# An eight-stage graph network and expert kernel: how edges are marked and in what order stages hand over

## The chip, the cores and the metric

The kernel runs on one core of one Trainium2 chip. The metric is device time in microseconds (us). Each number under "time" is one whole execution of the kernel; the median of three is given. One further execution was recorded by the profiler, and all rows come from it.

## What is computed

A residual network of four blocks over 1250 nodes with 1024 features each. The 21250 edges are sorted by destination. `LN` is a layer norm without scale and offset.

```python
# block 1: 4 hops of attention over the edges (row = source, col = destination)
x1  = LN(x) @ W1 + b1                                  # 1250 x 512
dis = clip(number of edges into a node, 1) ** -0.5
gnn = x1
for k in range(4):
    alpha = tanh(gnn[col] @ Wi[k] + gnn[row] @ Wj[k] + bg[k])       # one number an edge
    msg   = (dis[row] * dis[col])[:, None] * alpha[:, None] * gnn[row]
    gnn   = gnn + segment_sum(msg, col)
x = x + concat([x1, gnn], 1)
# block 2: dense layer, and for each node the best of 4 low-rank experts
x = x + LN(x) @ W.T + gate * (LN(x) @ Wd[top1].T @ Wu[top1].T)
# block 3: two layers of  h @ W_self + mean over incoming edges(h) @ W_neigh + b, relu between
x = x + sage(relu(sage(LN(x))))
# block 4: 8 experts; each takes its 313 best nodes by a router's softmax
for e in range(8):
    x[sel[e]] += gate[e] * (gelu(LN(x)[sel[e]] @ w1[e] + b1[e]) @ w2[e] + b2[e])
```

## The kernel before, in words

**Tiles.** Nodes stand in 10 tiles of 128 rows (padded to 1280). Weights and activations that are multiplied are split into two f16 parts, a high and a low one; a product of such pairs is three matmuls (high x high, low x high, high x low). Five instruction streams run beside one another and wait by semaphores: TensorE (`pe`), VectorE (`v`), ScalarE (`s`), GpSimd (`g`) and SyncE, whose stream issues most transfers.

**First stage (A).** For each node tile: layer norm (`ln` on ScalarE, coefficients on VectorE, low part `ln_low_a` on GpSimd), 16 transposes, 24 matmuls of 512 columns with W1 and 16 small ones with the attention vectors (`v1s`). Between the tiles' products stand the windows, from which the adjacency matrix is counted. A window is 50 destination nodes; 25 windows cover 1250. Edges lie in 170 chunks of 125. For each chunk a marking matrix is made twice: `oh_d` (125 edges x 500, one column for each pair of source tile and destination in the window) on VectorE by comparing a row of numbers (`iotaw`) with a code for each edge, and `oh_s` (125 x 128, the place of the source in its tile). A matmul of the two adds the chunk's edges into a bank of 500 columns. The code of an edge depends on the window: GpSimd works out 170 of them for each window (L672 to L674, three instructions). `oh_s` is made on ScalarE for three chunks of four (distance L1399, then L1408 or L1419) and on VectorE for the fourth (L1732). A window takes 4 chunks at first and 4 more in each further visit of a loop whose count is read from a table (L571 to L575): 27 visits in all. A last product with zeros (L1034) closes the bank, and ScalarE copies it into `adj` (L1425).

**Hops.** The adjacency matrix is dense: 10 source tiles x 1280 destinations. A hop is done in two halves of five destination tiles. For each source tile ScalarE makes tanh of the attention sum over 640 destinations (`th`, L1450), VectorE multiplies by the counts (`hm`, L1790), ScalarE copies to the high part (`hop`, L1455) and VectorE subtracts to the low part (L1795). TensorE does 150 products a half (L1075 to L1077) and, ahead of them, `chain` (L1097), 80 small products that bring the new attention sums; their row is copied by VectorE (`prow`, L1832), spread by TensorE (L1124). After each half the new features are formed on VectorE and ScalarE (L1804, L1462, L1808). `dinv_row` (1280 columns) is a reciprocal that the sums by destination are scaled with (L1827). Ahead of the first hop stand the degrees: a square root (L1472), the scaling of the first features (L1479) and the row of attention sums (L1439). From the first hop on GpSimd also loads and converts the weights of block 2 (`whole(a["ffnW"] ...)`, L645 to L647).

**Later stages.** Block 2 (B) and block 3 (C) follow with the same two-part products (L1159 to L1198) and statistics (L512); the order of steps at their borders is written out by hand in `staged_late` and `flow_late`. At the border of B and C the gates `zT` (L1959) come from VectorE, and tile 0 of C is loaded as `cx` by SyncE's queue (L856), behind the loads and stores of B (L808, L852). The router of block 4 has a chain of its own a tile: statistics, coefficients (L521 to L532), ScalarE `cy` (L544) and its f16 copy `dyh` (L547), GpSimd's low part (L536), transposes (L556).

## Time and profile before

| what | value |
|---|---|
| median of three runs | 1720.75 us (1716.56 to 1721.64) |
| the profiled execution | 1721.65 us, span 1720.0 us, mean granted TensorE clock 0.94 |
| TensorE matmul busy (PE) | 1515.6 us, 88% of the span |
| weight load (PEld, beside PE) | 813.7 us |
| VectorE (DVE) | 918.1 us, 53% |
| ScalarE (ACT) | 632.5 us, 37% |
| GpSimd (POOL) | 386.2 us, 22% |
| transfers | 158.16 MB, mean 92 GB/s |

The span is what the profiler's records cover; 1.65 us of the execution lie outside. A busy share is an average over the stages. The first 230 us hold the first stage and the way to the hops, about 229 to 580 the four hops, then B, from 730 C, from about 1390 the experts. In each row a name stands as out<-in by the program's names, xN is a count of instructions, and what stands behind `<-` in brackets is what released an engine that had been idle.

### The profile page before, as it was taken

Reading aid. Unit: us, or ns where it says so; the run is one execution under the profiler, and the core shown is the slowest. Engines: PE = TensorE matmul, PEld = TensorE weight load, DVE = VectorE, ACT = ScalarE, POOL = GpSimd, SP = SyncE. Lnnn points to the kernel's source line nnn. Section 1 sums busy time; section 2 is a strip of 40 time slices with the busy share of each in tenths; the row PEclk is TensorE's granted clock in tenths of the full one; section 3 lists DMA queues with packets and bytes.
Section 4 is the critical chain, followed back from the end, with each engine's and each line's share of the span. In section 5 each row is a group of like instructions: output and inputs, shape, how many; then the busy total and the mean of one; then the engine's idle time right before and its main releaser. Section 6 shows DMA issues by size and latency. Waiting matters only on the chain.

```text
span 1720.0 us, 30722 instructions
## 1 busy us (share of the span) xinstructions
PE 1515.6 (88%) x9054; PEld 813.7 (47%) x9054; DVE 918.1 (53%) x2102; ACT 632.5 (37%) x858; POOL 386.2 (22%) x355
## 2 busy tenths in 40 slices
PE   5788767799999998789999998999988925999996
PEld 4344334344445454344445444444544524766764
...
DMA packets 55685, 158.16 MB, mean 92 GB/s; under 512 B 6980, under 2 KB 8467, under 8 KB 55608
## 3 DMA queue, kind: packets, MB, share of 16 engines
...
q14 instruction: 36, 0.29, 0.1%
...
## 4 chain that ended last, share of the span: by engine, by line
PE 47%; issue 26%; DVE 13%; ACT 6%; POOL 3%; DMA 2%; ACTq 1%; DVEq 1%; SPq 0%; POOLq 0%
PE ps L1159 12%; PE ps L1346 7%; PE ps L1330 6%; PE ps L1230 5%; PE ps L1075 2%; PE ps L1076 2%; PE ps L1077 2%; PE ps L996 2%; PE ps L556 2%; DVE hm L1790 2%; ACT th L1450 2%; DVE gn L1804 1%; PE ps L1318 1%; DVE bstat L512 1%; POOL wa L647 1%
## 5 line engine op out<-in xcount | busy, mean ns | idle before, releaser
L1159 PE MATMUL ps<-wa,tb 128*128 128x512 f16 x960 | 214.3, 384 | 6.9 <-DVEq L2083 5.2
L1230 PE MATMUL ps<-adj,nm 128*128 128x512 f16 (+1 forms) x960 | 178.5, 345 | 2.9 <-DVEq L2042 1.6
L1075 PE MATMUL ps<-gp,hop 128*128 (+1 forms) x400 | 154.4, 386 | 29.7 <-DVE hop L1795 18.6
L1076 PE MATMUL ps<-gp,hop 128*128 (+1 forms) x400 | 154.0, 385 | 0.0
L1077 PE MATMUL ps<-gp,hop 128*128 (+1 forms) x400 | 153.9, 385 | 0.0
L1159 PEld LDWEIGHTS ps<-wa,tb 128*128 (+1 forms) x960 | 93.8, 99 | 119.6 <-issue 10.9
L1230 PEld LDWEIGHTS ps<-adj,nm 128*128 x960 | 93.4, 97 | 88.4 <-issue 4.4
L1547 ACT ACTIVATE tb<-cx 128x512 f32 (+1 forms) x48 | 26.8, 559 | 282.5 <-DVE cx L2032 282.5
L1346 PE MATMUL ps<-wa,hT 128*105 128x512 f16 x576 | 126.8, 379 | 1.7 <-issue 1.7
L1159 PE MATMUL ps<-wb,hop 128*128 128x512 f16 x480 | 109.2, 389 | 0.0
L1159 PE MATMUL ps<-wa,hop 128*128 128x512 f16 x480 | 106.6, 383 | 2.9 <-DVEq L1969 2.9
L1330 PE MATMUL ps<-tkT,wb 128*128 128x315 f16 x768 | 106.6, 300 | 1.1 <-ACT tkT L1593 1.1
L1159 PE MATMUL ps<-wb,tb 128*128 128x512 f16 x480 | 106.1, 385 | 1.4 <-ACT tb L1500 1.4
L1731 DVE TENSOR_SCALAR oh_d<-iotaw,code 125x500 f16 (+1 forms) x208 | 75.0, 422 | 43.1 <-POOL code L674 37.3
L1346 PEld LDWEIGHTS ps<-wa,hT 128*105 128x105 f16 x576 | 72.6, 128 | 50.2 <-issue 2.0
L1330 PEld LDWEIGHTS ps<-tkT,wb 128*128 128x128 f16 x768 | 75.2, 98 | 32.1 <-issue 1.3
L1790 DVE SCALAR_TENSOR_TENSOR hm<-adj,th 128x640 f32<-128x640 f32 x80 | 68.9, 903 | 37.0 <-ACT th L1450 35.6
L2032 DVE TENSOR_TENSOR cx<-ps,dinv_row 128x512 f32<-128x512 f32 (+1 forms) x48 | 29.0, 603 | 110.7 <-PE ps L1230 110.7
L536 POOL TENSOR_TENSOR dyh<-cy,dyh 128x1024 f16<-128x1024 f32 x10 | 21.2, 2124 | 271.5 <-ACT dyh L547 271.5
L1075 PEld LDWEIGHTS ps<-gp,hop 128*128 (+1 forms) x400 | 40.0, 100 | 78.6 <-issue 34.1
L1795 DVE TENSOR_TENSOR hop<-hm,hop 128x640 f32 x80 | 69.3, 908 | 13.7 <-ACT hop L1455 13.7
L1159 PEld LDWEIGHTS ps<-wb,tb 128*128 x480 | 47.5, 99 | 59.8 <-issue 4.7
...
## 6 DMA issues: line engine op xcount, KB each, us to landing
w_st<-in_ew SPq DMA_DIRECT2D x16, 2048.0 KB, 11.1
...
```

The costliest lines, as they stand in the source:

```text
L556: ins = pe.transpose(bank16(bank + part)[:, k * P:k * P + TP], y_[:, k * P:(k + 1) * P], ident16[0:TP, 0:TP])
L996: pe.matmul(ps[:, 2 + j, :], lhs, w1[:, w, k, :], start=(n == 0), stop=(n == 3 * KT - 1))
L1075: pe.matmul(acc, wh, gh, start=(s_ == 0), stop=False, skip_group_check=True)
L1076: pe.matmul(acc, wh, gl, start=False, stop=False, skip_group_check=True)
L1077: ins = pe.matmul(acc, wl, gh, start=False, stop=(s_ == NT - 1), skip_group_check=True)
L1159: ins = pe.matmul(ps[:, b + c, :], lhs(part, k), w[:, w_, k, c * 512:(c + 1) * 512], start=(k == 0 and part == 0 and w_ == 0), stop=(last ...
L1230: ins = pe.matmul(ps[:, 6 + j, 0:w_], nm[:, part, s_, bass.ds(f * P, P)], adj[:, s_, CC * c:CC * c + w_], start=(s_ == 0 and part == 0), s ...
L1330: ins = pe.matmul(ps[:, 2 + h, 0:3 * SLOT], w1b[:, j, w_, k * H + h * P:k * H + (h + 1) * P], tkT[:, j, part, k, :], start=(k == 0 and w_ ...
L1346: ins = pe.matmul(ps[0:SLOT, 6 + o, :], hT[:, part, h, c * SLOT:(c + 1) * SLOT], w2b[:, j, w_, h * D + o * 512:h * D + (o + 1) * 512], sta ...
L1731: v.tensor_scalar(dst[:, c], iotaw[:], at[:, c:c + 1], None, ALU.is_equal)
L1790: v.scalar_tensor_tensor(hm[:, j, :], tile_of(adj[:, :, h * HALF:(h + 1) * HALF], 2 * r + j), 2.0, th[:, j, :], ALU.mult, ALU.mult).then_i ...
L1795: v.tensor_tensor(tile_of(hop[:, h, 1], 2 * r + j).rearrange("p (d n) -> p d n", n=P)[:, :, 0:TP], hm[:, j, :].rearrange("p (d n) -> p d n ...
```

## The change

**Marks.** GpSimd's codes are gone. VectorE works out once, at the start, one number an edge (`key`, which holds window, source tile and place in the window); one number a window (`winbase`) comes from the index row. An edge is marked by one instruction with two per-partition numbers: `(iotaw + winbase[w]) is_equal key`. A window takes 6 chunks at first and 2 more in each visit (again 27 visits); ScalarE makes `oh_s` for 4 of the 6, VectorE for 2 of the 6 and for both of a visit. The last product of a window closes its bank, without the product with zeros.

**The first stage's order.** Windows are 2 a tile for the first five tiles and 3 a tile for the last five (`WINDOWS`). ScalarE writes the high part of the normed tile straight from `xt`; GpSimd makes the full one and the low one. The loads of W1 come in another order, the statistics of the tiles are spread over the stage, the small products with `v1s` stand between groups of others, degrees are counted in three parts.

**Seam to the hops.** The square root of the source scale is made on VectorE, five tiles first; GpSimd scales the first features (high part); the first half hop's tanh and products are written out right behind the last window, and ahead of the table loads and clamps. The reciprocal of `dinv_row` is done on 128 columns, and on 384 more in each of three hops. New features go copy by copy, with the low part one step behind. The weight conversion of GpSimd waits for its turn: a pair of slices each hop (`hop_turn`).

**Borders of B and C, router.** `staged_late` and `flow_late` have their steps in another order, and the router's chain takes `dyh` from ScalarE's first pass, while GpSimd makes `cy` and the low part. Its coefficients take three linked instructions fewer.

The order of instructions on VectorE in one window of the first stage, before: four marks `oh_d` and one `oh_s`, then the loop of visits with four marks and one `oh_s` each.

```order
L1731 TENSOR_SCALAR oh_d<-iotaw,code 125x500
L1732 REGISTER_ALU
L1732 TENSOR_SCALAR oh_s<-iota,slo 125x128
...
L1731 TENSOR_SCALAR oh_d<-iotaw,code 125x500
L1731 ISA
L1731 TENSOR_SCALAR oh_d<-iotaw,code 125x500
L1731 ISA
L1731 TENSOR_SCALAR oh_d<-iotaw,code 125x500
L1731 ISA
L1731 TENSOR_SCALAR oh_d<-iotaw,code 125x500
L1732 ISA
L1732 TENSOR_SCALAR oh_s<-iota,slo 125x128
```

The same place now. The marking matrix is printed as `wa`, since it lies in that tile's storage.

```order
L1778 TENSOR_SCALAR wa<-iotaw,winbase,key 125x500
L1780 REGISTER_ALU
L1780 TENSOR_SCALAR oh_s<-iota,slo 125x128
L1780 REGISTER_ALU
L1780 TENSOR_SCALAR oh_s<-iota,slo 125x128
...
L1778 TENSOR_SCALAR wa<-iotaw,winbase,key 125x500
L1778 ISA
L1778 TENSOR_SCALAR wa<-iotaw,winbase,key 125x500
L1780 ISA
L1780 TENSOR_SCALAR ohv_s<-iota,slo 125x128
L1780 ISA
L1780 TENSOR_SCALAR ohv_s<-iota,slo 125x128
```

Of the marks ahead of the loop only the last is shown. Four marks and one `oh_s` by VectorE became six and two, and a visit's four and one became two and two.

ScalarE from the last window to the hops, before: the eviction `adj`, a table load, the root `dis`, the scaling of five tiles of features `gp`, then the loop with its clamps, and the tanh `th` behind another table load.

```order
L1425 ACTIVATE adj<-ps 128x10x50 x2
L1472 ACT_TABLE_LOAD
L1472 ACTIVATE dis<-dcol 128x10
L1479 ACTIVATE gp<-gn,dis 128x512 x5
L1446 UNCONDITIONAL_BRANCH
L1446 ISA
L1450 ISA
L1450 ACT_TABLE_LOAD
L1450 ACTIVATE th<-arow,bcur 128x640
L1449 REGISTER_ALU
L1450 ISA
L1450 ACTIVATE th<-arow,bcur 128x640
```

The same place now:

```order
L1460 ACTIVATE adj<-ps 128x10x50
L1467 ACTIVATE arow<-ps 128x512 x2
L1467 ACTIVATE arow<-ps 128x256
L1460 ACTIVATE adj<-ps 128x10x50
L1473 ACTIVATE th<-arow,bcur 128x640 x2
L1478 ACTIVATE hop<-hm 128x640 x2
L1473 ACTIVATE th<-arow,bcur 128x640 x2
L1478 ACTIVATE hop<-hm 128x640 x2
L1473 ACTIVATE th<-arow,bcur 128x640 x2
L1478 ACTIVATE hop<-hm 128x640 x2
```

Root and features left ScalarE, the copies of the row of attention sums (`arow`) stand between the last two evictions, and the pairs of tanh and high part follow at once.

TensorE at the border of B and C, before. L1159 are the dense products, L1198 the low-rank experts (`zT` is the gate times the down product), L1191 the transposes of that, L556 the transposes of the next stage's input.

```order
L1191 MATMUL ps<-ident,zcat 48x128
L1159 MATMUL ps<-wa,hop 128x512 x48
L1198 MATMUL ps<-wus,zT 128x512 x2
L556 MATMUL ps<-ident,nm 128x128 x16
L1191 MATMUL ps<-ident,zcat 48x128
L1198 MATMUL ps<-wus,zT 128x512 x2
L1159 MATMUL ps<-wb,hop 128x512 x48
L556 MATMUL ps<-ident,nm 128x128 x16
L1159 MATMUL ps<-wb,hop 128x512 x48
```

The same place now (L1217 were L1159, L1256 L1198, L1249 L1191, L585 L556):

```order
L1249 MATMUL ps<-ident,zcat 48x128
L1217 MATMUL ps<-wa,hop 128x512 x48
L1256 MATMUL ps<-wus,zT 128x512 x2
L1249 MATMUL ps<-ident,zcat 48x128
L585 MATMUL ps<-ident,nm 128x128 x16
L1256 MATMUL ps<-wus,zT 128x512 x2
L1217 MATMUL ps<-wb,hop 128x512 x48
L585 MATMUL ps<-ident,nm 128x128 x16
L1217 MATMUL ps<-wb,hop 128x512 x48
```

The last transposed gate moved ahead of the transposes of C's first tile, so that these stand between it and the product that reads `zT`.

SyncE's queue there, before: stores of a tile (L852) and loads of the next (L808) in turn, then the first tile of C, `cx`.

```order
L852 DMA x_d<-cr 128x1024
L808 DMA cr<-x_d 128x512
L808 DMA cr<-xg_d 128x512
L852 DMA x_d<-cr 128x1024
L808 DMA cr<-x_d 128x512
L808 DMA cr<-xg_d 128x512
L860 DMA bias<-in_bs 128x1024
L856 DMA cx<-x_d 128x1024 x2
L852 DMA x_d<-cr 128x1024
```

The same place now (L901 was L852, L857 L808, L909 L860, L905 L856):

```order
L901 DMA x_d<-cr 128x1024
L857 DMA cr<-x_d 128x512
L857 DMA cr<-xg_d 128x512
L909 DMA bias<-in_bs 128x1024
L905 DMA cx<-x_d 128x1024 x2
L901 DMA x_d<-cr 128x1024
```

The loads of `cx` stand one store earlier than before.

The diff, cut to the parts that are spoken of:

```diff
-GC = 4
+GC, GV = 6, 2
+GA = 4
 PAIRS = NCH // 2
 assert PAIRS * 2 == NCH
-BATCHES = ((0, 2), (2, 6), (6, 10))
+BATCHES = ((0, 2), (2, 4), (4, 7), (7, 10))
+LOADS = ((0, 2), (2, 4), (4, 10))
 HALF = 5 * TP
 PROJ = 256
...
+WINDOWS = tuple(range(2 * t, 2 * t + 2) if t < 5 else range(3 * t - 5, 3 * t - 2) for t in range(NT))
...
-    tr_n(0, 0), ln_n(0, 1), work(last, 1)
-    stats_n(1), tr_n(0, 1), ln_n(1, 0), done_n()
-    for step, lag in steps:
-        if lag == 1:
-            step(last, 1)
+    tr_n(0, 0), ln_n(0, 1), work(last, 1), done_n()
+    ends = [step for step, lag in steps if lag == 1]
+    for step in ends[:-1]:
+        step(last, 1)
+    tr_n(0, 1)
+    for step in ends[-1:]:
+        step(last, 1)
+    stats_n(1), ln_n(1, 0)
...
-    store(2, 1), again(3, 0), store(3, 0), again(3, 1), ahead(0), store(3, 1), again(4, 0), ahead(1)
+    store(2, 1), again(3, 0), ahead(0), store(3, 0), again(3, 1), store(3, 1), again(4, 0), ahead(1)
...
-                step.link(v.tensor_tensor(z2, z, z, ALU.mult))
-                step.link(v.tensor_tensor(z2, z2, ve, ALU.mult))
+                if single:
+                    step.link(v.scalar_tensor_tensor(z2, z, ve, z, ALU.mult, ALU.mult))
+                else:
+                    step.link(v.tensor_tensor(z2, z, z, ALU.mult))
+                    step.link(v.tensor_tensor(z2, z2, ve, ALU.mult))
...
             def ln_low_a(t):
-                ln_low(g, A, 0, t, y, yh[:, t % 2, :], yl[:, t % 2, :])
+                j = t % 2
+                g.wait_ge(A.aff, 1 + sum(t >= t1 for _, t1 in BATCHES))
+                g.tensor_scalar(y[:, j, :], xt[:, t, :], lnv_a[:, 1, t:t + 1], lnv_a[:, 2, t:t + 1],
+                                ALU.mult, ALU.add).then_inc(A.y, 1)
+                g.wait_ge(A.y, t + 1)
...
-            def codes(w):
-
-                j = w % 2
-                if w >= 2:
-                    g.wait_ge(s_win, w - 1)
-                link(g.tensor_scalar(ctmp[:, j, :], dst_f[:], winneg[0:EP, w:w + 1], -1.0, ALU.add, ALU.max))
-                link(g.tensor_scalar(ctmp[:, j, :], ctmp[:, j, :], float(WIN), None, ALU.min))
-                g.tensor_tensor(code[:, j, 0:NCH], ctmp[:, j, :], shw[:], ALU.add).then_inc(s_code, 1)
-
...
+            def hop_turn(r):
+                if isinstance(r, int):
+                    g.wait_ge(s_hlo, NT * (2 * HOPS - 1) + 2)
+                else:
+                    g.wait_ge(s_abc, r + 2)
+                    g.sem_inc(s_tick, 1)
 
             g.wait_ge(s_hlo, 2 * NT + 2)
-            whole(a["ffnW"], wa, s_wf)
+            whole(a["ffnW"], wa, s_wf, turn=hop_turn)
...
+                    g.wait_ge(D_.aff, D_.r + 2 * r + j + 1)
+                    g.sem_inc(s_tick, 1)
+                    g.wait_ge(D_.lo, D_.m + 2 * r + j)
+                    g.sem_inc(s_tick, 1)
+                    g.tensor_scalar(cy[:, 0, :], cr[:, j, :], lnv[:, 1, j:j + 1], lnv[:, 2, j:j + 1],
+                                    ALU.mult, ALU.add).then_inc(D_.y, 1)
+                    g.wait_ge(D_.y, D_.n + 2 * r + j + 1)
+                    g.sem_inc(s_tick, 1)
...
-                pe.matmul(acc, zero16[:, 0:P], zero16[:], start=False, stop=True, skip_group_check=True).then_inc(s_win, 1)
-
-            turn_a(0)
...
+            turn_a(0)
+            for t in range(NT):
+                products(t)
+                if t == 7:
+                    degrees(0, 5, ps[:, 4, 200:210])
+                for w in WINDOWS[t]:
+                    if w == NWIN - 1:
+                        pe.wait_ge(s_abc, 1)
+                        broadcast_a((0, 1, 3))
+                        degrees(5, 8, ps[:, 2, :])
+                    window(w)
+                    if w == WINDOWS[t][0] and t + 1 < NT:
+                        turn_a(t + 1)
+            degrees(8, NT, ps[:, 2, :]), row_degrees()
...
             def ln(t):
-                j = t % 2
                 s.wait_ge(A.aff, 1 + sum(t >= t1 for _, t1 in BATCHES))
-                s.activation(y[:, j, :], xt[:, t, :], ACT.Identity, scale=lnv_a[:, 1, t:t + 1],
-                             bias=lnv_a[:, 2, t:t + 1]).then_inc(A.y, 1)
-                s.wait_ge(A.y, t + 1)
-                s.activation(yh[:, j, :], y[:, j, :], ACT.Copy).then_inc(A.hi, 1)
+                s.activation(yh[:, t % 2, :], xt[:, t, :], ACT.Identity, scale=lnv_a[:, 1, t:t + 1],
+                             bias=lnv_a[:, 2, t:t + 1]).then_inc(A.hi, 1)
 
...
+                for c in range(GA):
+                    ins = s.activation(dist[:, j, c, :], iota128[:], ACT.Abs, scale=-1.0, bias=at[:, c:c + 1])
+                ins.then_inc(s_dist, 1)
+                if w >= 2:
+                    s.wait_ge(s_win, w - 1)
                 s.wait_ge(s_dist, w + 1)
-                s.activation(oh_s[:, j, 0:GC - 1], dist[:, 0], ACT.Relu, scale=-1.0, bias=1.0).then_inc(s_ohs, 1)
...
+            s.wait_ge(s_A_st[0], 16 * 6)
+            for s_ in range(0, NT, 2):
+                tanh_of(s_, s_ % 2, 0, s_), tanh_of(s_ + 1, 1, 0, s_ + 1)
...
-                v.tensor_scalar(shw[:], shi[:], float(CW), 1.0, ALU.mult, ALU.add).then_inc(s_shw, 1)
...
+                link(v.scalar_tensor_tensor(key[:, 0:NCH], shi[:], float(CW), rest[:], ALU.mult, ALU.add))
+                link(v.scalar_tensor_tensor(key[:, 0:NCH], q_f[:], float(NT * CW), key[:, 0:NCH], ALU.mult, ALU.add))
...
-                def visit(chunk, dst, src):
-                    at, lo = code[:, j, bass.ds(chunk, GC)], slo[:, bass.ds(chunk, GC)]
-                    for c in range(GC):
-                        v.tensor_scalar(dst[:, c], iotaw[:], at[:, c:c + 1], None, ALU.is_equal)
-                    return v.tensor_scalar(src[:, GC - 1], iota128[:], lo[:, GC - 1:GC], None, ALU.is_equal)
-
-                v.wait_ge(s_code, w + 1)
+                def marks(chunk, n, n_s, dst, src):
+                    at, lo = key[:, bass.ds(chunk, n)], slo[:, bass.ds(chunk, n)]
+                    for c in range(n):
+                        v.tensor_scalar(dst[:, c], iotaw[:], winbase[0:EP, w:w + 1], at[:, c:c + 1], ALU.add, ALU.is_equal)
+                    for c in range(n_s, n):
+                        ins = v.tensor_scalar(src[:, c], iota128[:], lo[:, c:c + 1], None, ALU.is_equal)
...
-                visit(first, oh_d[:, j], oh_s[:, j]).then_inc(s_ohd, 1)
+                    v.wait_ge(s_win, w - 1)
...
+            edges(), stats(0, 2), coefficients(0), ranges()
             for c in range(4):
                 w1_low(c)
-            split_v1(), ranges()
...
+                for w in WINDOWS[t]:
+                    if w + 2 < NWIN:
+                        one_hots(w + 2)
+                if t == 0:
+                    stats(4, 7), coefficients(2)
+                if t in (1, 2, 3):
+                    stats(6 + t, 7 + t)
+                if t == 3:
+                    coefficients(3)
+                if t == 8:
+                    first_features(0, 5)
...
+            for s_ in range(0, NT, 2):
+                product_of(s_, 0, 0, s_), product_of(s_ + 1, 1, 0, s_ + 1)
+                low_of(s_, 0, 0, s_), low_of(s_ + 1, 1, 0, s_ + 1)
+                if s_ == 2:
+                    take_degrees(3, 5, NT, ps[0:TP, 2, :])
+                if s_ == 4:
+                    source_scale(5, NT)
+            first_features(5, NT)
...
+                evict(0)
+                for d in range(1, 5):
+                    evict(d)
                     if split:
-                        v.wait_ge(s_ghi, 10 * (k + 1) + t + 1)
-                        ins = v.scalar_tensor_tensor(tile_of(gp2[:, 1], ring * NT + t), gn[:, t, :], dis16[:, t:t + 1],
-                                                     tile_of(gp2[:, 0], ring * NT + t), ALU.mult, ALU.subtract)
+                        low(d - 1)
                 if split:
-                    ins.then_inc(s_gp, 1)
-
-            v.sem_inc(s_gev, 5)
-            v.sem_inc(s_hm, 2)
...
-            link(v.reciprocal(dinv_row[:], dinv_row[:]))
-            with step.loop(0, HOPS - 1, 5) as k:
+            v.wait_ge(s_rest, 1)
+            link(v.reciprocal(dinv_row[:, 0:P], dinv_row[:, 0:P]))
...
+                part = dinv_row[:, bass.ds(k * (3 * P) + P, 3 * P)]
+                link(v.reciprocal(part, part))
...
-                ln_coefficients(v, step, D_, mv[:, j:j + 1, :], lnv[:, :, j:j + 1])
+                ln_coefficients(v, step, D_, mv[:, j:j + 1, :], lnv[:, :, j:j + 1], True)
```

## Rows read from the trace of the kernel before

**Rows 1.** Busy time by stretches; columns: stretch, length, PE, PEld, DVE, ACT, POOL, PEclk, DMA, GB/s

```profile
41.00:181.00 140.00, 113.54 (x722) 55.10 (x720) 101.25 (x291) 100.80 (x220) 71.32 (x78) 0.93 0.06 20
...
229.00:362.50 133.50, 113.41 (x560) 52.36 (x563) 97.60 (x113) 64.27 (x90) 43.46 (x32) 0.90 0.10 32
362.45:434.99 72.54, 71.31 (x407) 34.29 (x407) 46.81 (x72) 37.86 (x53) 0.00 (x0) 1.00 0.00 0
```

**Rows 2.** VectorE's waits, 40 to 206; columns: us in total, times, longest.

```profile
DVE oh_d L1731 <- POOL code L674: 37.3, 11, 5.9
```

**Rows 3.** ScalarE's groups, 40 to 206; columns: busy us, mean ns, idle before.

```profile
L1399 ACT ACTIVATE dist<-iota,slo 125x128 f16 x81 | 26.7, 391 | 1.8 <-issue 0.4
L1425 ACT ACTIVATE adj<-ps 128x500 f16<-128x500 f32 x25 | 14.4, 577 | 21.3 <-PE ps L1034 21.2
L1376 ACT ACTIVATE y<-xt,lnv_a 128x1024 f32<-128x1024 f32 x8 | 9.8, 1231 | 2.2 <-DVE lnv_a L532 2.2
```

**Rows 4.** VectorE's timeline, marks; columns: start, duration.

```profile
124.69 1.11 DVE L1731 TENSOR_SCALAR oh_d<-iotaw,code 125x500 f16<-125x500 f16 x4
...
131.70 2.21 DVE L1731 TENSOR_SCALAR oh_d<-iotaw,code 125x500 f16<-125x500 f16 x4 [3.33 <-POOL code L674]
```

**Rows 5.** VectorE's timeline, two pointers and two tensors.

```profile
384.76 1.56 DVE L1795 TENSOR_TENSOR hop<-hm,hop 128x640 f32 x2 [0.32 <-ACT hop L1455]
...
1395.81 0.23 DVE L2100 TENSOR_SCALAR sc<-rtmp 128x8 f32<-128x8 f32 x1
1396.08 0.29 DVE L2126 TENSOR_SCALAR sc<-sc,live 128x8 f32<-128x8 f32 x1
```

**Rows 6.** TensorE's groups, 40 to 206, products with W1.

```profile
L996 PE MATMUL ps<-wa,yT 128*128 128x512 f16 x240 | 60.1, 390 | 0.0
```

**Rows 7.** Timeline of all engines, last window to first hop.

```profile
203.85 0.59 ACT L1425 ACTIVATE adj<-ps 128x500 f16<-128x500 f32 x1 [1.83 <-PE ps L1034]
...
218.31 1.28 ACT L1450 ACT_TABLE_LOAD   x1
...
223.03 1.28 ACT L1450 ACT_TABLE_LOAD   x1
...
228.88 0.60 PE L1075 MATMUL ps<-gp,hop 128*128 x1 [18.55 <-DVE hop L1795]
...
242.20 8.15 DVE L1827 RECIPROCAL dinv_row<-dinv_row 128x1280 f32<-128x1280 f32 x1
```

**Rows 8.** Timeline of TensorE and VectorE in the hops.

```profile
268.57 6.08 PE L1097 MATMUL ps<-hop,pp 128*32 128x384 f16 x80 [5.11 <-DVE hop L1795]
...
305.52 2.98 DVE L1795 TENSOR_TENSOR hop<-hm,hop 128x640 f32 x2 [0.31 <-ACT hop L1455]
...
362.45 3.43 PE L1097 MATMUL ps<-hop,pp 128*32 128x384 f16 x80
...
370.46 0.86 PE L1124 MATMUL ps<-sel,prow 128*128 128x32 f32 x6 [1.23 <-DVE prow L1832]
```

**Rows 9.** TensorE's waits, 206 to 362.

```profile
PE ps L1075 <- DVE gn L1804: 11.1, 1, 11.1
```

**Rows 10.** TensorE's waits, 670 to 729.

```profile
PE ps L1198 <- DVE zT L1959: 15.5, 2, 8.7
```

**Rows 11.** Timeline at the border of B and C.

```profile
678.34 2.49 DVE L512 BATCH_NORM_STATS2 bstat<-cx 128x6 f32<-128x512 f32 x4 [9.74 <-DMA cx<-x_d]
...
716.45 12.84 PE L1159 MATMUL ps<-wb,hop 128*128 128x512 f16 x48
```

**Rows 12.** TensorE's waits, 1276 to 1392.

```profile
PE ps L556 <- POOL dyh L536: 13.6, 2, 9.2
```

**Rows 13.** ScalarE's timeline in the router.

```profile
1384.84 1.24 ACT L544 ACTIVATE cy<-cr,lnv 128x1024 f32<-128x1024 f32 x1 [8.04 <-DVE lnv L532]
1386.11 1.06 ACT L547 ACTIVATE dyh<-cy 128x1024 f16<-128x1024 f32 x1
```

**Rows 14.** GpSimd's groups, whole span.

```profile
L645 POOL TENSOR_SCALAR stage<-stage 128x1024 f32<-128x1024 f32 x32 | 37.6, 1175 | 16.2 <-DMA stage<-in_wn 6.5 <-DMA stage<-in_ws 3.6 <-DMA stage<-in_ffnW 3.0
```

505 lines of the change are left out of this document (268 added, 237 removed).

## The prediction, made before the change was run

> **What bounds the kernel now.** I read the busy shares by stage first. Up to 204 us (the first stage: layer norm, first product, adjacency matrix) TensorE is busy for 114 of 140 us, VectorE and ScalarE for 101 each [rows 1]: nobody is full, all wait for one another in turn. In the first hop it is 113 in 133.5 [rows 1]; between the two lies a seam in which it stands nearly still. Then the waits, and the timeline where a wait is long. In the first stage VectorE waits 37.3 us for the codes of GpSimd [rows 2], and a window costs ScalarE six absolute distances of 0.39 us, two roundings and an eviction of 0.58 [rows 3]. So the stage ends by ScalarE and by VectorE waiting for codes, the hops by TensorE, once they run: from one chain product to the next 72.54 us, of which TensorE is busy 71.31 [rows 1]. Everything after 716 us is left as it was but for the router list.
>
> The profiled execution took 1721.65 us (span 1720.0, so 1.65 around it); the median of the three runs is 1720.75. I sum against 1721.65.
>
> **First stage.** What goes: 25 code triples of GpSimd; two of six distances a window and one rounding pass on ScalarE; the closing product with zeros (one of nine 500-column products); the `y` pass of ScalarE, 1.23 us a tile [rows 3], which GpSimd now makes beside it. What comes: VectorE makes four 128-wide one-hots a window instead of two, so 8 marks and 4 one-hots instead of 8 and 2 (the tables give 27 visits in either kernel: 208 marks before, 204 now).
>
> A mark is 0.28 us undisturbed (four in 1.11) and 0.55 beside GpSimd (four in 2.21) [rows 4]. The new mark reads two per-partition numbers. No row has it at this size. Bounds: nothing more than now, or what a second pointer adds on 8 columns, 0.29 against 0.23 [rows 5]; I take 0.03 for back-to-back issue, half of that, since the difference is partly latency. The far end is the loss of the fast mode: 640 float columns of two tensors took 1.56 for two, 0.78 each [rows 5], so some 0.65 for 500. The Trainium skill, "VectorE: DVE Perf Modes", section "Mode 4×_2P — both tricks at once", lets a second operation sit in slices of its own, so that it costs nothing; no run here shows it for two pointers. By that page the first stage would be 3 us shorter than I sum.
>
> Per tile then. TensorE: the 240 products took 60.1 us with slow stretches in it [rows 6]; 24 of them, by my estimate, 5.4, the small ones, now in a block, 0.4, transposes 1.2 and 1.7 a window: 10.4 with two windows, 12.1 with three. ScalarE: 3.2 a window (4 × 0.39, 0.58 and two roundings of about half a us), 1.0 + 1.23 for the tile [rows 3]: 8.7 or 11.9. VectorE: 2.9 a window, 0.7 + 0.7 + about 1.2 of statistics, some 2 for GpSimd's 4.7 us of work: 10.4 or 12.1. All three are level, and a third window must wait for its marks, which VectorE starts only after the transposed tile: 14 a tile. Start: the products began at 41 us, where the first stretch of [rows 1] does; VectorE must now work through keys, statistics, ranges, four weight parts of 1.23 and the first transposes: 38. First tile 6, then two of 15 (11, and 4 for the filling of the pipeline and the statistics of four tiles), to 74; three tiles of 11 to 107; four of 14, and 3 for degrees and features, to 166; the last windows with the broadcast 9; eviction and second pointers 3: last window evicted at 178. It was at 203.85 + 0.59 = 204.4 [rows 7]. **−26.4.** If the engines never waited for one another it would be 165; if the interleaving gains nothing over today's average of 14 a tile, 195.
>
> **Seam to the hops.** From that eviction to the first hop product, 228.88, it was 24.4 us [rows 7]: square root with its table load, feature scaling, row clamp, then three pairs of tanh and product. The root goes to VectorE beside it, the features to GpSimd, the first half hop is written out ahead of the clamps. A pair took 223.03 − 218.31 = 4.72, 1.28 of it a table load [rows 7], which the order has no more: 3.44. Three pairs, the first filling, 12.9. **−11.5.** Who comes late next: the second five sources need their features, at some 26 us after the eviction; TensorE is then on the first five until 31 (12.9, 16.2 for 75 products, 2 slow). Covered by 5.
>
> **Hops.** From the first product at 228.88 to the chain of the next hop at 362.45 it was 133.6 [rows 7, 8]. An undisturbed hop is 72.54 [rows 1], half a hop's 150 products (72.54 less the chain's 3.43 [rows 8] and some 4.5 of small ones, halved) 32.3: 104.8. The excess, 28.8, is the waits of 11.1 [rows 9] and 5.1 [rows 8], a shorter one, and slow clock after each: the same chain took 6.08 there and 3.43 here [rows 8]. The 5.1 comes from the reciprocal of 8.15 [rows 7] ahead of the second half; now 128 of 1280 columns stand there and 384 after each hop's columns (2.5). The 11.1 comes from GpSimd's weight conversion beside the next half: two subtractions took 2.98 [rows 8] instead of 1.56 [rows 5]. The conversion is spread: a pair of slices (12 us) after each hop's columns. SBUF — State Buffer in the Trainium skill, section "Who interferes with whom", has a VectorE operation with two SBUF inputs and a GpSimd one exclude each other for whole instructions; the trace agrees, by that doubling. So each pair still lies some 6.5 us on the next half: 3.4 later, but VectorE has 8 in hand there, since the features now go evict, evict, low without waiting for ScalarE (7 us for five, was 12.6). I leave 3 for the cold start: −25.8, and the row-copy wait of 1.23 [rows 8] in two later hops, which now has two products' blocks before it: −2.5. **−28.3.**
>
> **Seam from B to C.** TensorE waits twice for `zT`, 15.5 together [rows 10]. First 8.7: VectorE stood 9.74 for the load of `cx` [rows 11], which SP issued behind a store; that load moves ahead of the store of tile 7, ready 12 us earlier, so nothing waits, and the slow instructions behind it (1.6) go. Then 6.8: statistics were in front of the `zT` copy; they now follow it, and 48 products that took 12.84 after the idling [rows 11] take 10.5, by 0.215 each as in a hop. Together 19.8; the low part of the next tile is then just in time, for which I leave 0.8. **−19.**
>
> **Router.** TensorE waits for `dyh` twice, 13.6 [rows 12]; elsewhere the list is covered by 10.5 us of products. The chain loses the second pass (1.06 [rows 13]) and three linked operations of 0.2 on eight columns or fewer, as the 0.23 [rows 5]; GpSimd's multiply-add beside ScalarE's own 1.24 [rows 13] can at best be as fast as that and at worst 0.5 later (mean of the like in GpSimd 1.18 [rows 14]). 1.65 twice: **−3.3.** Each of the two could be up to 0.5 worse.
>
> Sum −26.4 − 11.5 − 28.3 − 19.0 − 3.3 = −88.5: **1633 us**.
>
> **Rivals.** (1) The first stage stays coupled: windows wait for marks in every tile, last window at 195 instead of 178. For it: three engines within 10% of each other, and 4.7 us of GpSimd a tile. Against: the long waits for codes are gone. 1650. (2) The conversions cost more than the slack: each of three hops 3.4 to 6 on the path, and the last pair lies on the last half hop, another 3. For it: TensorE is 98% busy in a hop, so all that is late shows. Against: VectorE is busy only 46.8 of 72.5 us there. 1648. (3) Marks at one column a cycle, 0.65: 204 × 0.37 = 75, less 15 for the slack that VectorE has in ScalarE's and TensorE's shadow: 1693. For it: a form that no row shows; against: the page above. (4) Slower: the same place, priced higher. VectorE starts each mark only when both pointers are read and the last mark has drained, 0.29 [rows 5] and an estimated 0.52 for 500 columns (the 0.65 above less latency), 0.81. From 0.80 a mark the sum is not negative: (88.5 + 15)/204 = 0.51 over 0.28. At 0.85 it is 1733. (5) The seams move on: the wait at `zT` is found again at the next tile's low part, and only half of the 19 comes: 1643.
>
> **Chances.** Forecast 0.58, (1) 0.14, (2) 0.10, (3) 0.06, (4) 0.03, (5) 0.09. The likeliest one's own range is 1615 to 1648 (stage end 168 to 188, seams and hops 5 either way). All unknown ends together, without (3) and (4) and the thin tails: 1608 to 1672. A measurement tells 0.3% (5 us): faster 0.95, same 0.02, slower 0.03; only (4) and something unseen of like size lie beyond.
>
> **What would show it.** First stage: no codes, VectorE's marks at 0.26 to 0.32 undisturbed, last adjacency eviction at 168 to 188. Seam: tanh right behind it, no table load in the first half hop, first hop product 13 later. Hops: no TensorE wait over 2 us between first hop product and last, and about 284 us of them in all. Seam B to C: no idle on VectorE for `cx` and both `zT` waits under 1 us. Router: last `dyh` wait near 7.5 instead of 9.2. I am wrong if marks take 0.4 or more alone, if TensorE waits for a half hop's low parts while GpSimd converts, or if the last eviction is later than 195.

## The result and the profile after

The changed kernel took 1677.3 us (median of four, 1671.2 to 1677.9), the kernel before 1719.8 in runs beside it: a ratio of 0.9747, with a 95% interval of 0.972 to 0.9774. It is 42 us faster where the forecast's sum was 88.5, and the time lies outside the range given, 1608 to 1672. The profiled execution has a span of 1675.9 us.

To see where the 44 us of the two spans come from I cut both at the same six instructions. Times are starts in the traces, in us (the products of C are taken to their end); the forecast's figure stands in the last column. An eviction is the copy of a finished bank of TensorE's results; the last one into `adj` ends the first stage.

| from ... to | before | after | change | forecast |
|---|---|---|---|---|
| start, last eviction into `adj` | 203.9 | 211.8 | +7.9 | −26.4 |
| that, first hop product | 25.0 | 11.3 | −13.7 | −11.5 |
| that, first dense product of B | 315.6 | 287.7 | −27.9 | −28.3 |
| that, end of C's products with its first `W_self` | 296.9 | 291.0 | −5.9 | −19.0 |
| that, last small product of the router | 551.6 | 546.8 | −4.8 | −3.3 |
| that, end | 327.0 | 327.3 | +0.3 | 0 |

Four rows came within 2.5 us of the forecast. Two did not, and they are the whole miss: the first stage by 34 us, the border of B and C by 13 (the others together gave 3 us more than forecast).

**The first stage.** Stretches of the profile after: start and end, length, then busy time and instructions of PE, PEld, DVE, ACT and POOL, the granted TensorE clock, DMA share, GB/s.

```profile
41.00:181.00 140.00, 101.76 (x644) 47.05 (x642) 120.17 (x321) 61.07 (x129) 45.98 (x28) 0.83 0.04 16
122.40:142.40 20.00, 15.80 (x82) 6.81 (x80) 14.88 (x38) 9.29 (x21) 5.10 (x3) 0.74 0.04 15
223.10:508.00 284.90, 281.87 (x1550) 134.87 (x1551) 224.35 (x335) 144.06 (x197) 51.78 (x37) 0.99 0.14 44
```

In the same 140 us VectorE is busy for 120 us instead of 101 [rows 1], ScalarE for 61 instead of 101, and TensorE for less, 102 instead of 114: the work that left ScalarE was not what held the stage. The second line is one tile with three windows: 20 us, where I had summed 14, at a granted clock of 0.74 of full speed. The third holds the four hops. The waits of TensorE up to 520 us (total, times, longest) name what it stood for:

```profile
PE ps L1051 <- DVE yT L592: 19.9, 4, 7.9
PE ps L1081 <- DVE oh_s L1780: 16.6, 6, 8.8
...
PE ps L1087 <- DVE ohv_s L1780: 6.1, 5, 2.4
```

All three are for VectorE: copies of the transposed tile (`yT`) and one-hots, with the marks ahead of them. (The only other one of that size is for a load of W1, ahead of 41 us.) A stretch of the timeline without GpSimd, then that tile, VectorE and GpSimd (start, duration):

```profile
99.98 2.00 DVE L1778 TENSOR_SCALAR wa<-iotaw,winbase,key 125x500 f16<-125x500 f16 x6
...
124.31 0.41 DVE L1780 TENSOR_SCALAR oh_s<-iota,slo 125x128 f16<-125x128 f16 x2
125.20 2.14 POOL L566 TENSOR_TENSOR yl<-y,yh 128x1024 f16<-128x1024 f32 x1 [12.41 <-ACT yh L1434]
125.28 3.34 DVE L1780 TENSOR_SCALAR ohv_s<-iota,slo 125x128 f16 x2
127.31 1.26 POOL L705 TENSOR_TENSOR xt<-xt,gn 128x512 f32<-128x512 f32 x1
128.54 2.86 DVE L1778 TENSOR_SCALAR wa<-iotaw,winbase,key 125x500 f16<-125x500 f16 x6
128.55 1.75 POOL L698 TENSOR_SCALAR y<-xt,lnv_a 128x1024 f32<-128x1024 f32 x1
```

Undisturbed, six marks take 2.00 us and the next instruction starts 1.92 after the first: 0.32 each, against 0.26 to 0.28 [rows 4]. The whole VectorE work of a window is 3.2 us (99.98 to 103.19), where I had 2.9. Two one-hots take 0.41 alone and 3.34 while GpSimd subtracts and adds: the first 2.12 beside the subtraction of 2.14, the second 1.30 beside the addition of 1.26. The next six marks take 2.86 beside its third pass.

The longest wait of the stage stands between the products of the eighth tile and of the ninth, where VectorE also works out the root of the source scale (the first line is its start) and GpSimd scales five tiles of features:

```profile
164.37 0.16 DVE L1828 TENSOR_SCALAR dtmp<-dtmp 128x5 int32<-128x5 int32 x1
...
168.30 5.48 DVE L1778 TENSOR_SCALAR wa<-iotaw,winbase,key 125x500 f16<-125x500 f16 x6 [1.50 <-issue]
...
171.32 8.10 POOL L709 TENSOR_SCALAR gp<-gn,dis 128x512 f16<-128x512 f32 x5
...
174.21 2.24 PE L1081 MATMUL ps<-wa,oh_s 125*128 125x500 f16 x5 [8.80 <-DVE oh_s L1780]
```

The step from tile to tile is 26.9 us there (152.1 to 179.0). The forecast had 3 us for degrees and features in all.

**Seam to the hops.** ScalarE and TensorE after the last window:

```profile
211.81 0.59 ACT L1460 ACTIVATE adj<-ps 128x500 f16<-128x500 f32 x1 [2.01 <-PE ps L1091]
212.30 1.54 ACT L1473 ACTIVATE th<-arow,bcur 128x640 f32<-128x640 f32 x2
215.44 1.53 ACT L1473 ACTIVATE th<-arow,bcur 128x640 f32<-128x640 f32 x2
...
223.14 0.39 PE L1127 MATMUL ps<-gp,hop 128*128 x1 [4.60 <-DVE hop L1809]
```

The tanh follows the eviction at once, a pair of them repeats after 3.14 us without a table load (4.72 with it [rows 7]), and the wait of 18.55 [rows 7] became one of 4.60.

**Hops.** TensorE's waits from the first hop product to B; the first line is the one just shown, ahead of the hops:

```profile
PE ps L1127 <- DVE hop L1809: 4.6, 1, 4.6
PE ps L1127 <- DVE gn L1894: 1.6, 3, 0.6
PE ps L1149 <- DVE hop L1809: 1.4, 1, 1.4
```

The waits of 11.1 [rows 9], 5.11 and 1.23 [rows 8] are gone.

**Border of B and C.** TensorE's waits from 640 to 690, and the timeline behind the last wait for `zT`:

```profile
PE ps L585 <- DVE nm L566: 10.4, 1, 10.4
PE ps L1256 <- DVE zT L2050: 0.8, 1, 0.8
```

```profile
666.02 10.53 PE L1217 MATMUL ps<-wb,hop 128*128 128x512 f16 x48
671.29 1.29 DVE L2057 SCALAR_TENSOR_TENSOR cr<-ps,cr 128x512 f32<-128x512 f32 x2 [5.35 <-DMA cr<-xg_d]
672.80 2.47 DVE L539 BATCH_NORM_STATS2 bstat<-cx 128x6 f32<-128x512 f32 x4 [0.22 <-DVE cr L2057]
681.11 2.12 POOL L678 TENSOR_TENSOR wa<-stage,wa 128x1024 f32 x1 [0.19 <-POOL wa L677]
681.17 2.09 DVE L561 TENSOR_SCALAR lnv<-lnv 128x2 f32<-128x2 f32 x1
687.00 1.89 PE L585 MATMUL ps<-ident,nm 128*128 128x128 f16 x16 [10.44 <-DVE nm L566]
688.68 11.87 PE L1217 MATMUL ps<-wb,hop 128*128 128x512 f16 x48
```

The two waits for `zT`, 15.5 us [rows 10], are 0.8, and a new one of 10.44 stands one tile further. It is followed back in three steps: VectorE's last eviction of B waited 5.35 us for the load of its tile, the statistics of C's next tiles stood behind it, and their small instructions then ran beside GpSimd's weight conversion (2.09 us for two columns). The 48 products behind the wait took 11.87 instead of 10.53.

**Router.**

```profile
PE ps L585 <- POOL dyh L566: 10.1, 2, 8.1
```

It was 13.6 [rows 12]: the two waits are 8.1 and 2.0 where they were 9.2 and 4.4.

### The profile page after: what moved, and what is told of

Same layout as the page of the kernel before. It is cut to its first block, busy times and chain, and to the rows that moved or that the text cites. A ratio compares the mean times of both kernels' runs of the same rounds, so it can differ in the third digit from the quotient of the medians.

```text
span 1675.9 us, 30048 instructions
## 1 busy us (share of the span) xinstructions
PE 1505.0 (90%) x9025; PEld 805.3 (48%) x9025; DVE 958.4 (57%) x2170; ACT 565.2 (34%) x739; POOL 376.2 (22%) x310
## 3 DMA queue, kind: packets, MB, share of 16 engines
q1 hardware_dynamic: 43704, 115.57, 19.4%
## 4 chain that ended last, share of the span: by engine, by line
PE 68%; DVE 16%; issue 8%; ACT 3%; DVEq 2%; DMA 1%; POOL 1%; ACTq 0%; SPq 0%; POOLq 0%
PE ps L1217 24%; PE ps L1288 11%; PE ps L1404 7%; PE ps L1388 6%; PE ps L1127 3%; PE ps L1128 3%; PE ps L1129 3%; PE ps L1051 2%; PE ps L585 2%; DVE hm L1804 1%; DVE wa L1778 1%; PE ps L1376 1%; DVE bstat L539 1%; ACT th L1473 1%; PE ps L1025 1%
## 5 line engine op out<-in xcount | busy, mean ns | idle before, releaser
L1217 PE MATMUL ps<-wa,tb 128*128 128x512 f16 x960 | 214.2, 384 | 6.9 <-DVEq L2174 5.2
L1127 PE MATMUL ps<-gp,hop 128*128 (+1 forms) x400 | 152.6, 381 | 6.2 <-DVE hop L1809 4.6
L1128 PE MATMUL ps<-gp,hop 128*128 (+1 forms) x400 | 152.5, 381 | 0.0
L1129 PE MATMUL ps<-gp,hop 128*128 (+1 forms) x400 | 152.3, 381 | 0.0
L1217 PEld LDWEIGHTS ps<-wa,tb 128*128 (+1 forms) x960 | 93.8, 99 | 119.4 <-issue 10.7
L1288 PEld LDWEIGHTS ps<-adj,nm 128*128 x960 | 93.4, 97 | 88.5 <-issue 4.3
L1217 PE MATMUL ps<-wa,hop 128*128 128x512 f16 x480 | 106.9, 383 | 2.7 <-DVEq L2060 2.7
L1217 PE MATMUL ps<-wb,hop 128*128 128x512 f16 x480 | 107.8, 386 | 0.0
L1217 PE MATMUL ps<-wb,tb 128*128 128x512 f16 x480 | 106.0, 385 | 1.4 <-ACT tb L1531 1.4
L1778 DVE TENSOR_SCALAR wa<-iotaw,winbase,key 125x500 f16<-125x500 f16 (+1 forms) x204 | 85.4, 479 | 8.7 <-issue 8.6
L1051 PE MATMUL ps<-wa,yT 128*128 128x512 f16 x240 | 66.4, 444 | 19.9 <-DVE yT L592 19.9
L2301 DVE SCALAR_TENSOR_TENSOR yb<-ps,adj 105x512 f32<-105x512 f32 x48 | 33.1, 691 | 78.7 <-PE ps L1404 78.7
L1217 PEld LDWEIGHTS ps<-wb,tb 128*128 x480 | 47.4, 99 | 59.7 <-issue 4.6
L1809 DVE TENSOR_TENSOR hop<-hm,hop 128x640 f32 (+1 forms) x80 | 69.0, 902 | 11.8 <-ACT hop L1478 11.5
L1217 PEld LDWEIGHTS ps<-wa,hop 128*128 128x128 f16 x480 | 46.6, 99 | 59.1 <-DVEq L2060 3.2
## 6 DMA issues: line engine op xcount, KB each, us to landing
w_st<-in_ew SPq DMA_DIRECT2D x16, 2048.0 KB, 10.4
```

The lines of the kernel that those rows point to most:

```text
L1051: pe.matmul(ps[:, 2 + j, :], yT[:, j, part, k, :], w1[:, w, k, :], start=(n == 0), stop=(n == 3 * KT - 1))
L1127: pe.matmul(acc, wh, gh, start=(s_ == 0), stop=False, skip_group_check=True)
L1128: pe.matmul(acc, wh, gl, start=False, stop=False, skip_group_check=True)
L1129: ins = pe.matmul(acc, wl, gh, start=False, stop=(s_ == NT - 1), skip_group_check=True)
L1217: ins = pe.matmul(ps[:, b + c, :], lhs(part, k), w[:, w_, k, c * 512:(c + 1) * 512], start=(k == 0 and part == 0 and w_ == 0), stop=(last ...
L1288: ins = pe.matmul(ps[:, 6 + j, 0:w_], nm[:, part, s_, bass.ds(f * P, P)], adj[:, s_, CC * c:CC * c + w_], start=(s_ == 0 and part == 0), s ...
```

## The experiments

All are timed beside the kernel before (1719.4 to 1719.9 us). "Eviction" is the start of the last one into `adj` in the profiled execution. Unless another is named, the edit is made to the changed kernel (1677.3 us, eviction 211.8). Three kernels below are not edited ahead of that eviction and had it at 209.6, 209.9 and 211.4, so a difference of some 2 us in it says nothing.

**The third window's one-hots ahead of the transposed tile.** "One-hots" here are all that VectorE makes for a window, the marks and the 128-wide matrices (function `one_hots`). Theories: O, the order; G, GpSimd stops VectorE; P, the second pointer.

```diff
+                early = t >= 5 and t + 1 < NT
+                if early:
+                    one_hots(WINDOWS[t][0] + 2)
                 if t + 1 < NT:
                     turned(t + 1)
...
-                    if w + 2 < NWIN:
+                    if w + 2 < NWIN and not (early and w == WINDOWS[t][0]):
                         one_hots(w + 2)
```

(and the same on ScalarE, `sources(w + 2)` ahead of `turned(t + 1)`.)

> The changed kernel with one order turned round, in tiles 5 to 8: VectorE and ScalarE make the one-hots of the first of the three next windows before they copy the transposed tile, not behind it. The changed kernel took 1677.3 us; its last adjacency eviction was at 212 us and a tile with three windows took 20 us (122.4 to 142.4). Theory O (order: the marks of the third window stand behind the copy of the transposed tile, so that TensorE, which has only two windows' buffers, waits for them ahead of the products): a tile falls to about 15, the eviction comes at 190 to 195, the kernel takes 1655 to 1660. Theory G (GpSimd's two passes over a tile stop VectorE) and theory P (the second pointer of 204 marks): VectorE's work is the same, so within 5 us of 1677.

Measured 1662.1 us, eviction 198.1: 13.7 of the 34 that were missing, so theory O, if some 3 us less than it said. From one tile's products to the next, from 109.4 on (110.7 in the changed kernel), it took 13.8, 19.4, 16.8 and 20.8 us instead of 19.6, 21.8, 26.9 and 14.8. What is left shows in its timeline: in one tile there is still this.

```profile
135.68 2.18 POOL L566 TENSOR_TENSOR yl<-y,yh 128x1024 f16<-128x1024 f32 x1 [7.50 <-ACT yh L1434]
135.81 3.33 DVE L1783 TENSOR_SCALAR ohv_s<-iota,slo 125x128 f16 x2
...
139.63 0.87 PE L1087 MATMUL ps<-wa,ohv_s 125*128 x2 [3.06 <-DVE ohv_s L1783]
```

**Marks with one pointer.**

```diff
-                        v.tensor_scalar(dst[:, c], iotaw[:], winbase[0:EP, w:w + 1], at[:, c:c + 1], ALU.add, ALU.is_equal)
+                        v.tensor_scalar(dst[:, c], iotaw[:], at[:, c:c + 1], None, ALU.is_equal)
```

> The changed kernel with marks that read one per-partition number instead of two: the window's number is left out, so that only the first window's edges are counted. A mark was 0.32 us undisturbed (six in 2.00 less the overlap) against 0.26 in the kernel before. Theory P: a mark falls back to 0.26, 204 x 0.06 = 12 us, all on the path: 1665. Theory O: VectorE's marks are on the path only where TensorE waits for them, about half: 1671. Theory G: no more than 1671 either, since the stalls stay.

Measured 1672.4, eviction 202.6. The stage gained 9.2 us of P's 12, more than O's half; 4 of them were lost again between B and the end of C's first products (295.1 us instead of 291.0), where nothing was edited. That part lay between 287.1 and 295.1 in all runs of the changed order at that border, and between 277.8 and 278.5 in those where it was turned (below).

**Without GpSimd's two passes over the tile.**

```diff
-                g.tensor_scalar(y[:, j, :], xt[:, t, :], lnv_a[:, 1, t:t + 1], lnv_a[:, 2, t:t + 1],
-                                ALU.mult, ALU.add).then_inc(A.y, 1)
-                g.wait_ge(A.y, t + 1)
-                ln_low(g, A, 0, t, y, yh[:, j, :], yl[:, j, :])
+                g.sem_inc(A.y, 1)
+                g.wait_ge(A.hi, A.m + t + 1)
+                g.sem_inc(A.lo, 1)
```

(and the low part is set to zero once, ahead of the tiles; the addition of 1.26 stays.)

> The changed kernel without GpSimd's full and low part of the normed tile in the first stage (1.75 and 2.14 us a tile): both passes are left out and the low part is zero; semaphores are raised as before. Theory G: VectorE loses its stalls, 3 us twice a tile (two one-hots in 3.34 instead of 0.41): 25 to 35 us earlier, 1645 to 1652. Theory O: the third window still waits behind the copy; what goes is one stall of 3 us on the path in each of five tiles and half of that in the others: 1660 or more. Theory P: no change in marks that are undisturbed.

Measured 1650.6, eviction 189.6: 22.2 us earlier, the kernel 26.7 shorter, as theory G had it. One group of VectorE's from 41 to 213, of this kernel and then of the changed one (count | busy us, mean ns | idle):

```profile
L1780 DVE TENSOR_SCALAR ohv_s<-iota,slo 125x128 f16 x54 | 14.0, 300 | 0.0
```

```profile
L1780 DVE TENSOR_SCALAR ohv_s<-iota,slo 125x128 f16 x54 | 20.5, 421 | 0.0
```

The edit also makes the low part ready sooner, and that could have been the gain. It was not: in the changed kernel the low part was done at least 2.9 us before its transposes began, in every tile (127.3 and 140.4 in the one above). The wait of 8.8 us ahead of the ninth tile's products is still 7.2 here, and GpSimd's scaling of features still runs beside it; no run took that away.

**Two windows a tile, seven at the end.** `WINDOWS` is `2t, 2t+1` for the first nine tiles and all the rest in the last.

> The changed kernel with two windows in each of the first nine tiles and seven behind the last, as the kernel before had it. Theory O: no third window in a tile, tiles of 14 us, the seven last at about 5 us each; last eviction near 202, kernel 1667. Theories G and P: VectorE's work is the same and it is what bounds the stage: last eviction at 212 or later, since the seven last windows have no product beside them; 1677 to 1685.

Measured 1665.7, eviction 199.7. Theory O again: a third window in a tile was worth less than nothing as it was ordered.

**Both edits of the first stage together.** No passes of GpSimd, and the third window's one-hots first.

> The changed kernel with both edits of the first stage: no GpSimd passes over the normed tile (the low part is zero) and the first next window's one-hots ahead of the copy of the transposed tile. Alone they moved the last adjacency eviction from 211.8 to 189.6 and to 198.1. If stalls and order are two causes, the gains add: 176, about where the forecast had put it, and the kernel takes 1677.3 - 26.7 - 15.2 = 1635. If they are one wait seen from two sides, the second adds 5 us or less: eviction at 185 or later, kernel at 1645 or more.

Measured 1638.0, eviction 176.7. The gains add: 22.2 and 13.7 alone, 35.1 together. They are two causes. The marks and one-hots of a window now follow one another without a gap or a stall:

```profile
119.58 2.01 DVE L1781 TENSOR_SCALAR wa<-iotaw,winbase,key 125x500 f16<-125x500 f16 x6 [0.36 <-PE ps L1091]
121.51 0.41 DVE L1783 TENSOR_SCALAR oh_s<-iota,slo 125x128 f16<-125x128 f16 x2
121.83 0.72 DVE L1781 TENSOR_SCALAR wa<-iotaw,winbase,key 125x500 f16 x2
```

**The kernel before with the marks alone.** The diff is the change's own for marks and key; GpSimd's codes are not called, all else is as before.

> The kernel before with one part of the change alone: VectorE marks by one key an edge and the window's number (two pointers), GpSimd makes no codes; visits of four chunks, loads, order, seams and hops are as before. Before: last adjacency eviction at 203.9, kernel 1719.6. Theory F (the 37.3 us that VectorE waited for codes are on the path): it is left with 208 x 0.06 = 12 us more of marks and without the stalls by codes: last eviction near 185, kernel at 1700. Theory C (the stage is coupled; behind the codes the next wait, for TensorE's windows and ScalarE's one-hots, ends 5 us or less earlier): eviction at 197 or later, kernel at 1713 or more.

Measured 1723.2 in ten runs (ratio to before 1.0022, 1.0012 to 1.0031), eviction 205.7: slower, if anything. VectorE's waits from 40 to 206:

```profile
DVE oh_d L1740 <- PE ps L1029: 9.8, 2, 6.2
DVE gn L1714 <- PE ps L998: 8.4, 5, 3.7
DVE oh_d L1740 <- issue: 6.6, 8, 1.4
DVE oh_d L1740 <- PE ps L1020: 6.0, 7, 1.8
```

The wait of 37.3 us for codes [rows 2] is gone, and 24 us of waits for TensorE stand there, where the kernel before had 4.7 (and 3.5 for the degrees at the end of the stage); marks and one-hots are busy for 104 us instead of 90. Theory C held: codes exchanged for marks with two numbers give the stage nothing. What the end of the wait is worth without the dearer marks was not run. One number less a mark gave 9.2 us in the changed kernel, so it may be about that, and not 37.

**The border of B and C: statistics ahead of the last eviction.**

```diff
     tr_n(0, 1)
+    stats_n(1)
     for step in ends[-1:]:
         step(last, 1)
-    stats_n(1), ln_n(1, 0)
+    ln_n(1, 0)
```

> The changed kernel with one step moved at the border of B and C: the statistics of C's tiles 2 and 3 (four of 0.62 us, then the linked coefficients) stand ahead of B's last eviction on VectorE, not behind it. In the changed kernel that eviction waited 5.35 us for a load, the statistics came after it, and TensorE then waited 10.4 us for the low part of C's third tile. From B's first dense product to the end of those of C's first layer it took 291 us. Theory S (order): the wait of 10.4 goes and the slow clock behind it: 279 us, kernel at 1665. Theory W (GpSimd's weight conversion for C, which starts at the same time and stops VectorE's small instructions, is what makes them late): the conversion still meets them, so 4 us at most: 1673.

Measured 1662.9, and 277.8 us for the part that took 291.0: −13.2, theory S, and the part that the forecast had for this border and that was missing. Its timeline:

```profile
663.89 2.45 DVE L540 BATCH_NORM_STATS2 bstat<-cx 128x6 f32<-128x512 f32 x4
...
669.33 1.28 DVE L2058 SCALAR_TENSOR_TENSOR cr<-ps,cr 128x512 f32<-128x512 f32 x2
...
674.41 1.06 PE L586 MATMUL ps<-ident,nm 128*128 128x128 f16 x16
```

The statistics start as the tile's products do (664.04), not 6.8 us behind them, the coefficients are done before GpSimd's conversion begins at 670.58, the eviction finds its load there, and TensorE's transposes stand without a wait. The linked coefficients take 2.9 us there (666.49 to 669.41), 7.9 in the changed kernel beside the conversion (675.43 to 683.32): of the wait of 10.4, 5 us were GpSimd's stalls, met only because the statistics were late.

**The hops: conversion at one stretch.** `whole(a["ffnW"], wa, s_wf)` without `turn=hop_turn`.

> The changed kernel with GpSimd converting the weights of B at one stretch from the first hop on, as the kernel before did, instead of a pair of slices each hop. From the first hop product to B's first dense product it took 287.7 us, before 315.6. Theory H (the conversion stops VectorE, and in the kernel before that was the wait of 11.1 us for new features and the slow clock behind it): the hops take 300 or more, kernel at 1690. Theory E (new features, copied one by one, now come early enough to hide it): 288 to 291, kernel at 1678 to 1681.

Measured 1691.1, hops 302.6 instead of 287.7. TensorE's longest wait from 205 to 560:

```profile
PE ps L1127 <- DVE gn L1894: 15.2, 1, 15.2
```

**The hops: the whole reciprocal first.** `v.reciprocal(dinv_row[:], dinv_row[:])`, and none in the loop.

> The changed kernel with the reciprocal of all 1280 columns (8.15 us before) ahead of the second half hop, instead of 128 columns there and 384 in each hop. Theory H (it is the wait of 5.1 us that the kernel before had at the chain products, and slow clock behind it): the hops take 294 to 296 us instead of 287.7, less 0 for the parts, which lie beside products: kernel at 1684. Theory E (the first half hop is now written out ahead of it and TensorE has enough to do): 288 to 290, kernel at 1678.

Measured 1684.4, hops 297.6. Theory H in both cases; here a little more than it said. TensorE's longest wait in the same stretch:

```profile
PE ps L1149 <- DVE hop L1809: 8.6, 1, 8.6
```

**Both orders, with the whole computation.** The third window's and the statistics'.

> The changed kernel with the two orders turned round, the third window's and that of the statistics at the border of B and C; the whole computation is there. They lie in different stages, so the gains add: 1677.3 - 15.2 - 14.4 = 1648. A rival: the border's gain depended on how the loads fell there, and 5 to 8 us of it are lost: 1654.

Measured 1650.3 (ratio to before 0.9591, 0.957 to 0.9612), eviction 197.4. The two gains add to 27.0 of 29.6 us; the border part took 278.5.

**The full tile on ScalarE, and then the low part on VectorE.** Both on top of both orders, from tile 2 on. GpSimd's passes that are replaced are left out; the second block is added only for the second kernel.

```diff
             # ScalarE, ln(t)
+                if t >= 2:
+                    s.activation(y[:, t % 2, :], xt[:, t, :], ACT.Identity, scale=lnv_a[:, 1, t:t + 1],
+                                 bias=lnv_a[:, 2, t:t + 1]).then_inc(A.y, 1)
             # VectorE, behind a tile's one-hots (second kernel)
+                if t + 2 < NT:
+                    v.wait_ge(A.y, t + 3)
+                    ln_low(v, A, 0, t + 2, y, yh[:, t % 2, :], yl[:, t % 2, :])
```

> Both orders, and ScalarE makes the full normed tile (1.23 us) behind the high part from tile 2 on; GpSimd keeps only the subtraction of 2.14 us and the addition of 1.26. Theory G1 (each us of GpSimd's work beside marks stops VectorE): 45% of the two passes' 22 us go: last eviction near 188, kernel at 1638. Theory G2 (only GpSimd's instruction with two tensors stops VectorE; the pass with one tensor and two pointers costs it nothing): no change to both orders alone, 1647 to 1650.

Measured 1646.6, eviction 194.8 against 197.4: far from G1 and next to G2. The kernels' intervals (0.954 to 0.9584, and 0.957 to 0.9612) overlap, and 2.6 us of eviction is hardly more than kernels with the same first stage differ by, so they are not told apart. G2 is not shown word for word either: six marks took 2.86 instead of 2.00 beside that very pass (128.54, above).

> As with the full tile on ScalarE, and the low part's subtraction on VectorE from tile 2 on (1.22 us of its own in place of GpSimd's 2.14), so that GpSimd has only the addition of 1.26 left. Theory G: the stalls of GpSimd's subtraction (about 3 us a tile, two one-hots in 3.34 instead of 0.41) go and 1.22 come: against the full tile on ScalarE alone 8 x 1.7 = 14 us less on VectorE, of which about half show: 1632 to 1636. Rival: VectorE's own subtraction stands in line ahead of the marks that TensorE waits for, and it is even or slower: 1640 or more.

Measured 1644.2 (ratio 0.956, 0.9542 to 0.9577), eviction 192.0: the fastest that computes everything, 33 us below the changed kernel, though not told apart from the one above by its interval. The rival held. The one-hots' stalls are gone (mean 243 ns in that group, 421 in the changed kernel) and its wait has come: TensorE, 30 to 215, waits for the low part, which VectorE makes behind a tile's marks.

```profile
PE ps L586 <- DVE yl L567: 24.4, 7, 7.7
```

## Why the prediction was half right

**Marks: right in size, wrong in what they free.** A mark is 0.32 us undisturbed; I had 0.31. The fast mode held, so rivals (3) and (4) are out (their prices start from 0.28 a mark though the sum already held 0.31, some 6 us too much; it changes nothing). Wrong is the reading that the stage ends by VectorE's 37.3 us for codes [rows 2]. The kernel before with the marks alone shows it: no gain, 14.7 us more of marks and one-hots and 19.5 more of waits for TensorE in the place of the wait. I had even priced rival (1), the coupled stage, at 195, and given it 0.14; a last eviction later than 195 was one of my signs of being wrong, and it came at 211.8.

**First stage, "14 a tile": failed in two terms, 34 us.** Per tile I summed each engine, found them level and took 14, a little over the largest. That leaves out who stands behind whom. With two sets of window buffers the third window's marks can only begin when the first window is done, and VectorE took the copy of the transposed tile first, which waits for TensorE's transposes; then the marks ran with TensorE waiting (2.2 us for a window's first six, at 124.83 and 144.85) and the next tile's products not begun. That is 13.7 us, shown by turning the order. The second term is "some 2 for GpSimd's 4.7 us". The stall is whole instructions: 3 us for two one-hots that need 0.41. I had it as 2 us of VectorE's busy time a tile; without them my sum would have fallen hardly at all, since TensorE (10.4 and 12.1) was as long. But taking away two of GpSimd's three passes gave 22.2 us in the stage: a stall ahead of the one-hots that TensorE waits for is a delay in the chain, and no busy time that another engine hides. The Trainium skill, "SBUF — State Buffer", section "Who interferes with whom", says that a VectorE instruction in a mode with both ports and a GpSimd instruction shut each other out for the whole instruction, and it lists `tensor_scalar`, which marks and one-hots are, among those that can enter such a mode. I had used its rule for two-input instructions in the hops and not for these. The trace agrees: 0.41 against 3.34 with one tensor read. With both terms taken out the eviction came at 176.7, where the forecast had 177.5 for its start; its third tile ended at 74.8 (forecast 74), its sixth at 112.0 (107). That agreement is partly luck, since my sum still held 2 us a tile for GpSimd; what holds that kernel at 10 to 15 us a tile, and at 19.0 in the one with the feature scaling, was not separated further. So the two causes are shown; that they are all of the miss is not.

**Slow clock as the multiplier.** Where TensorE stands in every tile, its granted clock over the tile was 0.74, and the 24 products behind the waits took 7.68 us at 130.31, at a granted clock of 0.69; the same 24 took 5.35 with the order turned (123.17), at 1.00. I had counted the clock in the hops; here I had 5.4 for all of them.

**Seam to the hops: right.** 11.3 from the start of the last eviction, forecast 13.5; a pair takes 3.14 where I had 3.44.

**Hops: right, by the mechanisms named.** −27.9 for −28.3. The two edits that undo a part each brought back its wait: 8.6 us and 9.9 in the hops for the reciprocal, 15.2 and 14.9 for the conversion at one stretch. Neither was hidden by the earlier features. Rival (2) is out.

**Border of B and C: rival (5), and more than its half.** The two `zT` waits fell to 0.8 as forecast. Failed is "the low part of the next tile is then just in time, for which I leave 0.8": it was 10.4 late. I had followed `cx` and `zT` through the new order, and not the last eviction. Its load is issued behind the store of the tile before, as it always was: at 665.83, and before at 709.81. Before, TensorE's wait of 6.80 for `zT` covered it: the product that the eviction needs began 7.9 us after the eviction ahead (707.57, 715.50). Now it begins 1.9 us after it (663.59, 665.50), so the load shows, and the statistics stood behind it. Moving them ahead gave 13.2 us.

Before, and then after:

```profile
707.57 1.29 DVE L1966 SCALAR_TENSOR_TENSOR cr<-ps,cr 128x512 f32<-128x512 f32 x2 [2.64 <-PE ps L1198]
...
715.50 1.01 PE L1198 MATMUL ps<-wus,zT 48*128 48x512 f16 x2 [6.80 <-DVE zT L1959]
```

```profile
663.59 1.29 DVE L2057 SCALAR_TENSOR_TENSOR cr<-ps,cr 128x512 f32<-128x512 f32 x2 [2.63 <-PE ps L1256]
...
665.50 0.59 PE L1256 MATMUL ps<-wus,zT 48*128 48x512 f16 x2 [0.78 <-DVE zT L2050]
```

The sum there was also a little off: 8.7, 1.6, 6.8 and 2.3 are 19.4, and not 19.8.

**Router: right.** −4.8 over that part for −3.3; its two waits fell by 3.5, though by 1.1 and 2.4 and not by 1.65 each. Where the other 1.3 us come from was not followed.

Rivals (1) and (5) both came true. By their prices, 17 and 9.5 us, they would have been 1660 together, inside the range. It is 1677 because both were priced too low: they cost 34 and 13.
